# Two-layer graph network on 16 groups of four graphs: the first turn's convolution as 17 single taps, with a new opening order, and three moves inside the steps

## The chip, the cores and the metric

The kernel runs on one core of one Trainium2 chip. The metric is the device time of one execution in microseconds; the time before is the median of three runs. The profile is that of one further execution.

## The reference, cut to what matters

For 64 graphs of 128 nodes and 128 features:

```
h  = relu(layernorm(x))
# layer 0
c  = relu(bn1(conv1(hT)))                 # a 128x128 product, hT is [128 features, 128 nodes]
xc = relu(bn2(conv2(c)) + hT)             # 17 taps over the nodes, 128x128 each, zero pads of 8
s  = h @ w_se.T + b_se                    # 3 coordinates per node
A  = exp(-(|s_n|^2 + |s_m|^2 - 2 s_n.s_m))
nm = A @ relu(h @ w_msg.T + b_msg)
r, z, n: gates of [xc, nm] @ w_ih.T and h @ w_hh.T;  x = x + (1 - z) n + z h
# layer 1
x  = x + adj @ (relu(layernorm(x)) @ W) + b
```

Every product of layer 0's convolutions and gates is made as three products of numbers split into a high and a low part (high by high, high by low, low by high).

## The kernel before, in words

Four graphs are a group (512 columns), there are 16 groups, and two groups p and q are a turn, so there are 8 turns (NS). Each of the engines has its own list of instructions, written out by hand; they meet by semaphores. PE's list (L277 to L583) is `opening()`, then `step(t)` for t = 1 to 7, then `ending()`. A step finishes the state of the turn before (groups pp, qq: turned back by `o_turn`, second layernorm, `adj_h2`, `layer2`), does the convolution and the gates of its own turn (p, q), and does for the next turn (a, b) what lies ahead of a convolution: `x_turn` (transpose of the normalised x), `conv1`, `messages` (messages and the three coordinates), `rows_turn`, `distances`, `neighbour_sums`.

The second convolution (L284 `product`) is not made of 17 taps. The nodes are taken in four phases (node number modulo 4), and phases and taps are combined in sums and differences, so that for the four output phases nine products of four or five tap weights do. Each product is on 256 columns (8 graphs of 32 nodes), and each of its taps is three matmuls: 40 taps, 120 matmuls a turn. It needs sums of weights (M12, M22, M32, M21, M23; POOL L1190 to L1197), differences of phases (`pre`, POOL L825: five instructions into px), and sums of the results (`scaled_first`, `between`, `scaled_third`, POOL `sums` L1210: four instructions). `split_hi` (ACT L587) and `split_lo` (DVE L928) split the phases and their differences in five parts; `round_w` (ACT L592) and `split_w` (DVE L934) split the 37 tap weights in five parts, once.

Other helpers that the prediction speaks of: `hidden` (ACT L605) and `hidden_lo` (DVE L879) read the bank in which x was turned, and conv1 waits for them; `pairs` (DVE L885) copies the coordinates out of the bank of the messages (L890) and builds with eight or nine small instructions the rows that `rows_turn` transposes; `left_rows` (ACT) and `right_rows` (DVE L909) fill what `distances` multiplies; `decay`, `masked` (L919) give the attention; `conv_out`, `conv_round`, `conv_lo_out` finish the convolution for `gates_c`; `blend_start`, `candidate`, `blend_end` (L939 to L954) make the state that `o_turn` transposes; `residual` (L956) adds it to x; `normalise1`, `shift1` (L848), `scale1` (POOL L1151) and `first` (ACT L596) are the first layernorm of groups to come; `keep_clock(n)` (L299) issues n products of the identity that nobody reads.

In the order before, POOL's `opening()` waits for `pair_set` 4 (the last rows of coordinates of the first four groups) ahead of its five `pre` for turn 1 (L1235), and every step does the same (L1248).

Of the kernel before, what the change touches and what calls it, by code (L numbers as in the profile page):

```python
# [38 lines left out]
def gnn_kernel(nc, x_in, adj_in, vec_in, early_in, conv_in, gate_in, late_in, bias_in, out):  # L39
    ctx = ExitStack()  # L40
    with ctx:
# [68 lines left out]
        sv = sb("sv", [128, GG, S + 1])  # L110
# [115 lines left out]
        CX_FILLS = (0, 1, 2, 4, 4)  # L226

        def cx_source(k):
            return c1[:, 3:4] if k == 0 else px[:, CX_PARTS[k][0]:CX_PARTS[k][1]]

# [3 lines left out]
        def _(sp):  # L234
# [18 lines left out]
            load_x(4)  # L253
            for g in range(4, ARING):
                load_adj(g)
# [22 lines left out]
        def _(pe):  # L278
# [5 lines left out]
            def product(acc, side, x, weights):  # L284
# [5 lines left out]
                return last  # L290

# [161 lines left out]
            def opening():  # L453
                pe.wait_ge(ident_set, 1)
                keep_clock(17)
                x_turn(0)
                x_turn(1)
                keep_clock(9)
                conv1(0)
                conv1(1)  # L460
                messages(0)
                pe.wait_ge(w_split, 1)
                pe.wait_ge(cxlo_set, 1)
                product(pP, 0, X22, four(M22, True))
                messages(1)
                rows_turn(0)
                pe.wait_ge(w_split, 2)
                pe.wait_ge(cxlo_set, 2)
                product(pP, 1, X12, four(M12, True)).then_inc(f_done[0], 1)
                distances(0)  # L470
                rows_turn(1)
                pe.wait_ge(w_split, 3)
                product(pQ, 0, X21, four(M21, True))
                x_turn(2)
                distances(1)
                neighbour_sums(0)
                pe.wait_ge(cxlo_set, 3)
                product(pQ, 1, X23, four(M23)).then_inc(f_done[1], 1)
                conv1(2)
                messages(2)  # L480
                x_turn(3)
                neighbour_sums(1)
                pe.wait_ge(s1_set, 1)
                product(pP, 0, X32, four(M32)).then_inc(f_done[2], 1)
                conv1(3)
                messages(3)
                pe.wait_ge(w_split, 5)
                pe.wait_ge(cxlo_set, 5)
                pe.wait_ge(t_set, 1)
                product(pQ, 0, X11, four(A0, True))  # L490
                rows_turn(2)
                product(pQ, 1, X13, four(A2)).then_inc(f_done[3], 1)
                distances(2)
                pe.wait_ge(s32_set, 1)
                rows_turn(3)
                product(pP, 0, X31, four(A1))
                distances(3)
                neighbour_sums(2)
                product(pP, 1, X33, four(A3)).then_inc(f_done[4], 1)
                neighbour_sums(3)  # L500
                for g in range(2):
                    gates_h(g)
                    gates_n(g)
                    gates_c(g)

            def step(t):
                a, b, p, q, pp, qq = 2 * t + 2, 2 * t + 3, 2 * t, 2 * t + 1, 2 * t - 2, 2 * t - 1
                front, middle = t + 1 < NS, t < NS
                if front:
                    x_turn(a)  # L510
                o_turn(pp)
                if middle:
                    have(pe, cxlo_set, 5 * t + 1)
                    have(pe, ct_set, 2 * t)
                    product(pP, 0, X22, four(M22, True))
                if front:
                    conv1(a)
                    messages(a)
                    x_turn(b)
                if middle:  # L520
                    have(pe, cxlo_set, 5 * t + 2)
                    product(pP, 1, X12, four(M12, True)).then_inc(f_done[0], 1)
# [11 lines left out]
                if middle:  # L534
                    have(pe, cxlo_set, 5 * t + 3)
# [4 lines left out]
                if middle:  # L540
                    have(pe, s1_set, t + 1)
# [5 lines left out]
                if middle:  # L547
                    have(pe, cxlo_set, 5 * t + 5)
                    have(pe, t_set, t + 1)
                    product(pQ, 0, X11, four(A0, True))  # L550
# [5 lines left out]
                if middle:  # L556
                    have(pe, s32_set, t + 1)
# [28 lines left out]
        def _(act):  # L586
            def split_hi(t, k):  # L587
                have(act, c1_set if k == 0 else pre_set, 2 * t + 2 if k == 0 else 5 * t + CX_PRES[k])
                have(act, f_done[CX_FILLS[k]], t)
                act.activation(cx_hi[:, CX_PARTS[k][0]:CX_PARTS[k][1]], cx_source(k), ACT.Copy).then_inc(cxhi_set, 1)  # L590

# [19 lines left out]
            def conv1_out(g):  # L611
# [4 lines left out]
                if g % 2 == 0:  # L616
                    have(act, pre_set, 5 * (g // 2) - 2)
                    have(act, cxlo_set, 5 * (g // 2) - 4)
# [69 lines left out]
            def scaled_third(t):  # L688
                have(act, f_done[2], t + 1)
# [4 lines left out]
            def gates(t):  # L694
# [4 lines left out]
                if t + 1 < NS:  # L699
# [5 lines left out]
                if t == 0:  # L705
                    first(4)
                    first(5)
                hidden_gate(q)
                reset_gate(q)
                update_gate(q)  # L710

            def opening():
                act.dma_start(vec[:], vec_in).then_inc(vec_loaded, 16)
                act.dma_start(late[:], late_in).then_inc(late_loaded, 16)
# [8 lines left out]
                conv1_out(0)  # L723
                round_w(0)
                conv1_out(1)
                split_hi(0, 0)
                messages(0)
                round_w(1)
                split_hi(0, 1)
                left_rows(0)  # L730
                messages(1)
                round_w(2)
                decay(0)
# [576 lines left out]
```

## Time and profile before

| | us |
|---|---|
| median of three runs | 376.99 (376.59 to 378.67) |
| the profiled execution, its time | 378.42 |
| the profiled execution, its span | 376.5 |
| busy: PE / DVE / ACT / POOL | 341.2 / 286.4 / 208.7 / 174.1 |
| granted TensorE clock, mean | 0.964 |

In 40 slices of the span (9 is 90% busy or more; the clock in tenths of full):

```profile
PE   5758776979999999999999999999999999989864
DVE  4596688797878997797879887889767987653572
POOL 7763247212890179224951298118911594072022
PEclk9886889998999999999999999999999999999998
```

A slice is 9.4 us. The steps have regular length from slice 10 on; ahead of it lie the opening and the first step. A matmul's record is longer than the time until the next one starts, so what a stream of matmuls costs is read from their starts.

### The profile page before, as it was taken

Reading aid. Unit: us, or ns where it says so; the run is one execution under the profiler, and the core shown is the slowest. Engines: PE = TensorE matmul, PEld = TensorE weight load, DVE = VectorE, ACT = ScalarE, POOL = GpSimd, SP = SyncE. Lnnn points to the kernel's source line nnn. Section 1 sums busy time; section 2 is a strip of 40 time slices with the busy share of each in tenths; the row PEclk is TensorE's granted clock in tenths of the full one; section 3 lists DMA queues with packets and bytes.
Section 4 is the critical chain, followed back from the end, with each engine's and each line's share of the span. In section 5 each row is a group of like instructions: output and inputs, shape, how many; then the busy total and the mean of one; then the engine's idle time right before and its main releaser. Section 6 shows DMA issues by size and latency. Waiting matters only on the chain.

```text
span 376.5 us, 6337 instructions
## 1 busy us (share of the span) xinstructions
PE 341.2 (91%) x2212; PEld 311.8 (83%) x2212; DVE 286.4 (76%) x737; ACT 208.7 (55%) x403; POOL 174.1 (46%) x140
## 2 busy tenths in 40 slices
PE   5758776979999999999999999999999999989864
PEld 5757776769998899889988999889988998989663
DVE  4596688797878997797879887889767987653572
ACT  1545733576854686548744785468645835262242
POOL 7763247212890179224951298118911594072022
PEclk9886889998999999999999999999999999999998
DMA  7700020000220013000310031001100010000001
GB/s 256 275 3 0 0 66 20 0 1 2 86 83 2 1 58 113 0 0 30 105 36 1 2 112 57 0 2 65 49 1 2 0 57 1 3 28 30 0 0 57
DMA packets 7951, 15.10 MB, mean 40 GB/s; under 512 B 1008, under 2 KB 1648, under 8 KB 7792
## 3 DMA queue, kind: packets, MB, share of 16 engines
q1 hardware_dynamic: 7632, 14.56, 11.1%
q8 instruction: 18, 0.29, 0.3%
q10 hardware_dynamic: 288, 0.14, 0.1%
q14 instruction: 13, 0.11, 0.1%
HBM read 10.50 MB, written 4.19 MB: 39 GB/s over the span
## 4 chain that ended last, share of the span: by engine, by line
issue 40%; POOL 28%; PE 13%; DVE 11%; ACT 5%; DMA 1%; SPq 0%; POOLq 0%; DVEq 0%; ACTq 0%
POOL rs L1161 3%; POOL ac L838 3%; POOL px L842 3%; POOL base L1213 3%; POOL x_ring L1203 3%; POOL base L1215 3%; POOL px L832 3%; POOL px L840 2%; POOL px L835 2%; POOL base L1219 2%; POOL rs L1156 2%; ACT hn L601 1%; DMA x_ring<-x_in 1%; DVE cx_lo L931 1%; DVE st L855 1%
## 5 line engine op out<-in xcount | busy, mean ns | idle before, releaser
L1161 POOL TENSOR_TENSOR rs<-ve,neg_half 128x4 f32<-128x4 f32 x16 | 16.1, 1009 | 103.8 <-DVE ve L972 103.8
L280 PE MATMUL pP<-cx_hi,conv_hi 128*128 128x256 f32 x176 | 54.4, 309 | 5.6 <-DVE cx_lo L931 5.6
L281 PE MATMUL pP<-cx_lo,conv_hi 128*128 128x256 f32 x176 | 52.0, 296 | 0.0
L282 PE MATMUL pP<-cx_hi,conv_lo 128*128 128x256 f32 x176 | 52.0, 296 | 0.0
L280 PE MATMUL pQ<-cx_hi,conv_hi 128*128 128x256 f32 x144 | 46.0, 319 | 2.7 <-issue 2.2
L281 PE MATMUL pQ<-cx_lo,conv_hi 128*128 128x256 f32 x144 | 43.2, 300 | 0.0
L282 PE MATMUL pQ<-cx_hi,conv_lo 128*128 128x256 f32 x144 | 43.1, 299 | 0.0
L1156 POOL TENSOR_TENSOR rs<-ve,neg_half 128x8 f32<-128x8 f32 (+1 forms) x9 | 14.9, 1656 | 56.5 <-DVE ve L862 56.5
L280 PEld LDWEIGHTS pP<-cx_hi,conv_hi 128*128 128x128 f32 x176 | 34.4, 195 | 6.0 <-DVE conv_lo L936 3.5
L931 DVE TENSOR_TENSOR cx_lo<-px,cx_hi 128x576 fp32r<-128x576 f32 x32 | 35.0, 1116 | 0.6 <-ACT cx_hi L590 0.6
L282 PEld LDWEIGHTS pP<-cx_hi,conv_lo 128*128 128x128 f32 x176 | 34.3, 195 | 0.0
L281 PEld LDWEIGHTS pP<-cx_lo,conv_hi 128*128 128x128 f32 x176 | 34.3, 195 | 0.0
L280 PEld LDWEIGHTS pQ<-cx_hi,conv_hi 128*128 128x128 f32 x144 | 28.9, 201 | 3.5 <-issue 2.3
L649 ACT ACTIVATE work<-work,nb,rs 128x128 f32<-128x128 f32 x60 | 24.7, 482 | 10.5 <-DVE nb L976 10.5
L281 PEld LDWEIGHTS pQ<-cx_lo,conv_hi 128*128 128x128 f32 x144 | 28.9, 201 | 0.0
L282 PEld LDWEIGHTS pQ<-cx_hi,conv_lo 128*128 128x128 f32 x144 | 28.8, 200 | 0.0
L669 ACT ACTIVATE work<-pNR,rz_b 128x512 f32<-128x512 f32 x16 | 11.0, 686 | 31.2 <-PE pNR L282 31.2
L1203 POOL TENSOR_TENSOR x_ring<-work,late 128x512 f32<-128x512 f32 x16 | 23.0, 1440 | 11.2 <-DVE pair L907 11.2
L992 DVE SCALAR_TENSOR_TENSOR xc_lo<-base,xc_hi 128x512 fp32r<-128x512 f32 x16 | 17.1, 1066 | 12.1 <-ACT xc_hi L659 12.1
L942 DVE SCALAR_TENSOR_TENSOR work<-work 128x512 f32<-128x512 f32 x16 | 11.9, 744 | 17.1 <-ACT work L669 17.1
L922 DVE TENSOR_TENSOR att<-att,adj_ring 128x512 f32<-128x512 f32 x16 | 23.1, 1445 | 2.2 <-ACT att L640 1.8
L601 ACT ACTIVATE hn<-x_ring,nb,rs 128x128 f32<-128x128 f32 x56 | 22.3, 481 | 0.7 <-DVE nb L868 0.7
(246 smaller groups left out, 1022.3 us busy)
## 6 DMA issues: line engine op xcount, KB each, us to landing
x_ring<-x_in SPq DMA_DIRECT2D x16, 256.0 KB, 2.6
adj_ring<-adj_in SPq DMA_DIRECT2D x16, 256.0 KB, 3.3
out<-x_ring SPq DMA_DIRECT2D x15, 256.0 KB, 2.0
work<-conv_in SPq DMA_DIRECT2D x1, 1088.0 KB, 7.5
x_ring<-gate_in SPq DMA_DIRECT2D x1, 576.0 KB, 7.9
out<-x_ring SPq DMA_DIRECT2D x2, 128.0 KB, 1.7
work<-bias_in SPq DMA_DIRECT2D x1, 132.0 KB, 7.4
early<-early_in SPq DMA_DIRECT2D x1, 129.5 KB, 2.9
```

The source lines that it names most:

```text
L280: pe.matmul(acc, w_hi, m_hi, start=start, stop=False)
L281: pe.matmul(acc, w_hi, m_lo, start=False, stop=False)
L282: return pe.matmul(acc, w_lo, m_hi, start=False, stop=stop)
L601: last = act.activation(graph(hn[g % 2], j), xs(g, j), ACT.Identity, bias=nb1[:, i:i + 1], scale=rs1[:, i:i + 1])
L649: last = act.activation(graph(h2[g % 2], j), graph(x1[g % 2], j), ACT.Relu, bias=nb2[g % 2][:, j:j + 1], scale=rs2[g % 2][:, j:j + 1])
L922: dve.tensor_tensor(att[g % 2], att[g % 2], adjs(g), ALU.mult).then_inc(att_set, 1)
L931: dve.tensor_tensor(cx_lo[:, part], cx_source(k), cx_hi[:, part].bitcast(F32), ALU.subtract)\
L942: dve.scalar_tensor_tensor(cand[g % 2], tr, 1.0, cand[g % 2], ALU.add, ALU.mult).then_inc(rh_set, 1)
L992: dve.scalar_tensor_tensor(xc_lo[:, 2 * e:2 * e + 2], base[e][:], 0.0, xc_hi[:, 2 * e:2 * e + 2].bitcast(F32), ALU.max, ALU.subtract)\
L1156: pool.tensor_tensor(rs1[:, lane], ve1[:, lane], neg_half[:, lane], ALU.pow).then_inc(rs1_set, 1)
L1161: pool.tensor_tensor(rs2[g % 2][:], ve2[g % 2][:], neg_half[:, 0:GG], ALU.pow).then_inc(rs2_set, 1)
L1203: pool.tensor_tensor(xs(g).rearrange("p (g d) -> p g d", g=GG), x1[g % 2].rearrange("p (g d) -> p g d", g=GG), l1_bias, ALU.add).then_inc( ...
```

## The change

What it does:

1. **The first turn's convolution** is made by `direct(tap)`: 17 single taps on the split phases themselves. The high and low phases are stored in the order 0, 2, 1, 3 (SLOT), so that two phases are one operand of 512 columns where they lie side by side, and two of 256 where they don't. For turn 0 this drops the nine products, POOL's five `pre` and four `sums`, ACT's five `split_hi`, two `scaled_first` and `scaled_third`, DVE's five `split_lo` and `between`. It adds two `split_hi_phases`, two `residual_phases` (ACT) and two `split_lo_phases` (DVE). POOL's sums of weights move behind `scale1([2, 3])`, the weights are split in six parts with the plain taps first, and turn 1's parts are split in the order 0, 3, 4, 1, 2.
2. **The opening's lists** of all four engines and the loads' order are new. `pairs` is cut in `coordinates` (the copy out of the bank, into one of two sv) and `pair_rows` (the rest). POOL no longer waits for `pair_set` 4 ahead of turn 1's `pre`.
3. **In the steps**: `x_turn` of the next turn's first group moves from the step's start into q's gates (between `gates_h(q)` and `gates_n(q)`), with `hidden` and `hidden_lo`; `o_turn(p)` moves between `gates_n(q)` and `gates_c(q)`, with `residual(p)` ahead of `normalise1` on DVE; `x_turn(b)` moves ahead of `conv1(a)`; part 2 of the next turn's phases is split in the gates; POOL's `sums` move ahead of `with_bias(qq)` and of `pre` 2 and 3.

The diff outside the opening, cut to its core:

```diff
-        W_PARTS = (taps(5, T16), taps(8, M12), taps(8, M21), taps(8, A0), taps(8, A2))
-        W_SUMS = (2, 2, 3, 0, 0)
+        W_PARTS = (taps(8, A0), taps(8, A2), taps(1, T16), taps(4, M22), taps(8, M12), taps(8, M21))
+        W_SUMS = (0, 0, 0, 2, 2, 3)
...
+        FIRST_ORDER = (0, 3, 4, 1, 2)
+
+        SLOT = (0, 2, 1, 3)
...
             load_x(0)
+            load_x(1)
             sp.dma_start(early[:], early_in).then_inc(early_loaded, 16)
-            load_x(1)
...
             load_x(4)
+            sp.dma_start(late[:], late_in).then_inc(late_loaded, 16)
...
+            def direct(tap, start=False, stop=False):
+                w = T16 if tap == 16 else 4 * (tap % 4) + tap // 4
+                w_hi, w_lo = conv_hi[:, w * D:(w + 1) * D], conv_lo[:, w * D:(w + 1) * D]
+                ends = []
+                for e, bank in enumerate((pQ, pP)):
+                    at_even, at_odd = e + tap, e + 2 + tap
+                    slots = [SLOT[at_even % 4], SLOT[at_odd % 4]]
+                    if slots[1] == slots[0] + 1 and at_even // 4 == at_odd // 4:
+                        parts = [(bank[:], slice(slots[0], slots[0] + 2), at_even // 4)]
+                    else:
+                        parts = [(bank[:, 0:CG * QN], slice(slots[0], slots[0] + 1), at_even // 4),
+                                 (bank[:, CG * QN:], slice(slots[1], slots[1] + 1), at_odd // 4)]
+                    for acc, phases, at in parts:
+                        m_hi, m_lo = cx_hi[:, phases, :, at:at + QN], cx_lo[:, phases, :, at:at + QN]
+                        ends.append((pe.matmul(acc, w_hi, m_hi, start=start, stop=False),
+                                     pe.matmul(acc, w_hi, m_lo, start=False, stop=False),
+                                     pe.matmul(acc, w_lo, m_hi, start=False, stop=stop)))
+                return ends
...
-                if front:
-                    x_turn(a)
-                o_turn(pp)
...
                 if front:
+                    x_turn(b)
                     conv1(a)
                     messages(a)
-                    x_turn(b)
...
                     gates_h(q)
+                    if t + 2 < NS:
+                        x_turn(a + 2)
                     if not front:
                         o_turn(p)
                     gates_n(q)
+                    if front:
+                        o_turn(p)
                     gates_c(q)
...
+            def residual_phases(e):
+                act.wait_ge(hT_set, 2)
+                act.activation(base[e][:], own(0, e), ACT.Identity, bias=bn_b[:, 1:2]).then_inc((sumE_set, sumO_set)[e], 1)
...
                 hidden_gate(q)
+                if t + 2 < NS:
+                    hidden(p + 4)
                 reset_gate(q)
...
+                if 0 < t < NS - 1:
+                    split_lo(t + 1, 2)
                     split_lo(t + 1, 3)
                     split_lo(t + 1, 4)
                 blend_start(p)
...
                 blend_end(p)
+                if t + 2 < NS:
+                    hidden_lo(p + 4)
+                if t + 1 < NS:
+                    residual(p)
                 if t + 3 < NS:
                     normalise1([p + 6, p + 7])
...
                 blend_start(qq)
-                if front:
-                    hidden_lo(a)
-                residual(pp)
                 blend_end(qq)
+                normalise2(pp)
+                if front:
+                    coordinates(a)
+                    hidden_lo(b)
+                    pair_rows(a)
```

The opening after the change, engine by engine, with the calls joined on lines. PE:

```
keep_clock(15); x_turn(0); keep_clock(3); x_turn(1); conv1(0); conv1(1); messages(0); keep_clock(6)
wait w_split 1, cxlo_set 2
direct(0); direct(4); direct(8); messages(1); direct(12); direct(1); direct(5); rows_turn(0)
direct(9); x_turn(2); direct(13); rows_turn(1); distances(0)
wait w_split 2
direct(2); conv1(2); distances(1); messages(2); x_turn(3); direct(6); neighbour_sums(0)
direct(10); conv1(3); neighbour_sums(1); direct(14); messages(3); rows_turn(2); direct(3)
distances(2); direct(7); rows_turn(3); direct(11); distances(3); neighbour_sums(2); direct(15)
wait w_split 3
direct(16); gates_h(0); neighbour_sums(3); gates_n(0); gates_c(0)
gates_h(1); x_turn(4); gates_n(1); o_turn(0); gates_c(1)
```

ACT, from `conv1_out(0)` on:

```
conv1_out(0); round_w(0); conv1_out(1); split_hi_phases(0); split_hi_phases(1); round_w(1); round_w(2)
messages(0); residual_phases(0); messages(1); residual_phases(1); gate_hi; first(2); left_rows(0)
hidden(2); first(3); left_rows(1); decay(0); round_w(3); conv1_out(2); round_w(4); hidden(3)
decay(1); sums_hi(0); messages(2); round_w(5); conv1_out(3); sums_hi(1); messages(3)
left_rows(2); decay(2); split_hi(1, 0); split_hi(1, 3); left_rows(3); split_hi(1, 4); decay(3)
sums_hi(2); conv_round(0, 0); hidden_gate(0); conv_round(0, 1); first(4); sums_hi(3)
reset_gate(0); update_gate(0); candidate(0); split_hi(1, 1); split_hi(1, 2)
hidden_gate(1); hidden(4); first(5); reset_gate(1); update_gate(1)
```

DVE, from `split_w(0)` on:

```
split_w(0); split_lo_phases(0); split_lo_phases(1); coordinates(0); split_w(1); normalise1([2, 3])
split_w(2); pair_rows(0); coordinates(1); shift1([2, 3]); pair_rows(1); right_rows(0)
hidden_lo(2); right_rows(1); masked(0); split_w(3); coordinates(2); split_w(4); hidden_lo(3)
masked(1); pair_rows(2); sums_lo(0); gate_lo; split_w(5); coordinates(3); right_rows(2)
sums_lo(1); pair_rows(3); masked(2); right_rows(3); normalise1([4, 5]); masked(3); sums_lo(2)
conv_out(0, 0); shift1([4, 5]); split_lo(1, 0); conv_lo_out(0, 0); conv_out(0, 1)
split_lo(1, 3); conv_lo_out(0, 1); sums_lo(3); split_lo(1, 4); blend_start(0)
split_lo(1, 1); split_lo(1, 2); blend_end(0); hidden_lo(4); residual(0); normalise1([6, 7])
```

POOL: `scale1([0])` and `scale1([1])` are moved between the small instructions of the biases, so that the sums of weights lie behind them:

```
wait cxlo_set 2; scale1([2, 3]); the three sums of weights; pre(1, 1) to pre(1, 5); scale1([4, 5])
```

## Rows read from the trace of the kernel before

**Rows 1.** Stages, all engines: window, its length, busy us of each engine, clock, DMA.

```profile
19.80:78.46 58.66, 46.51 (x258) 41.38 (x259) 47.45 (x118) 31.51 (x59) 23.21 (x15) 0.85 0.05 14
78.46:121.98 43.52, 40.96 (x270) 37.72 (x269) 35.70 (x105) 27.44 (x55) 21.04 (x15) 0.96 0.11 38
202.98:243.49 40.51, 39.82 (x269) 36.55 (x268) 33.53 (x91) 25.50 (x50) 20.50 (x15) 1.00 0.12 40
```

**Rows 2.** Waits of PE between 17.1 and 79.2 us: total, times, longest.

```profile
PE pP L280 <- DVE cx_lo L931: 5.6, 2, 3.3
```

**Rows 3.** Stages at the lower clock, same columns as rows 1.

```profile
25.20:35.50 10.30, 7.51 (x31) 6.68 (x32) 9.16 (x18) 4.48 (x10) 6.10 (x4) 0.51 0.01 2
42.30:45.70 3.40, 3.40 (x18) 3.40 (x17) 2.14 (x4) 1.68 (x4) 1.28 (x1) 0.51 0.00 0
52.50:56.00 3.50, 3.50 (x19) 3.50 (x18) 2.80 (x12) 0.87 (x2) 0.73 (x1) 0.52 0.45 137
83.30:86.70 3.40, 2.75 (x10) 2.50 (x11) 3.25 (x13) 0.78 (x1) 0.00 (x0) 0.50 0.02 5
```

**Rows 4.** Waits of PE, first 79.2 to 125 us, then 125 to 324 us.

```profile
PE pH L280 <- DVE h_lo L882: 2.6, 1, 2.6
...
PE pH L280 <- issue: 1.8, 5, 0.4
PE pH L280 <- DVE h_lo L882: 1.5, 5, 0.3
```

**Rows 5.** PE in order of time: start, us, line, shape: 256 columns, then 512.

```profile
20.61 0.30 PE L280 MATMUL pP<-cx_hi,conv_hi 128*128 128x256 f32 x1
20.75 0.30 PE L281 MATMUL pP<-cx_lo,conv_hi 128*128 128x256 f32 x1
...
67.10 0.40 PE L280 MATMUL pZ<-h_hi,gate_hi 128*128 128x512 f32 x1
67.33 0.40 PE L281 MATMUL pZ<-h_lo,gate_hi 128*128 128x512 f32 x1
```

**Rows 6.** DVE, then PE, in order of time, up to the first product.

```profile
12.49 0.69 DVE L882 SCALAR_TENSOR_TENSOR h_lo<-pI,h_hi 128x512 fp32r<-128x512 f32 x1 [0.34 <-ACT hT L609]
...
14.43 0.77 PE L280 MATMUL pH<-h_hi,early_hi 128*128 128x512 f32 x1
...
19.80 0.36 PE L280 MATMUL pP<-cx_hi,conv_hi 128*128 128x256 f32 x1 [2.30 <-DVE cx_lo L931]
```

**Rows 7.** DVE's groups by line over the whole span: ns min/median/max.

```profile
L936 DVE TENSOR_TENSOR conv_lo<-work,conv_hi x5: 824/1218/1560, 17.2 to 42.4; 128x1024 fp32r<-128x1024 f32 x4, 128x640 fp32r<-128x640 f32 x1
...
L931 DVE TENSOR_TENSOR cx_lo<-px,cx_hi x32: 748/758/1967, 25.6 to 315.9; 128x576 fp32r<-128x576 f32 x32
```

**Rows 8.** DVE (first three), then POOL, in order of time.

```profile
46.38 0.69 DVE L892 TENSOR_TENSOR sq<-sv 128x12 f32<-128x12 f32 x1
...
47.31 1.02 DVE L896 CAST svx<-sv 128x16 fp32r<-128x16 f32 x1
...
48.91 0.17 DVE L907 COPY pair<-svx 128x8 f32<-128x8 f32 x1
...
45.75 1.29 POOL L1215 TENSOR_TENSOR base<-base,s 128x512 f32<-128x512 f32 x1
47.00 1.29 POOL L1219 TENSOR_TENSOR base<-base,hT 128x512 f32<-128x512 f32 x1
...
57.99 1.88 POOL L838 TENSOR_TENSOR ac<-c 128x576 f32<-128x576 f32 x1
```

**Rows 9.** DVE, then PE, in order of time, around the start of step 4.

```profile
199.83 1.64 DVE L855 BATCH_NORM_STATS2 st<-x_ring 128x6 f32<-128x128 f32 x8
...
202.57 0.69 DVE L942 SCALAR_TENSOR_TENSOR work<-work 128x512 f32<-128x512 f32 x1 [0.22 <-ACT work L669]
...
213.69 0.69 DVE L914 TENSOR_TENSOR right<-pF,vec 64x512 fp32r<-64x512 f32 x1
...
215.39 0.39 PE L374 MATMUL pF<-right,left 128*128 128x512 f32 x1
```

More of the change, by code:

```diff
@@ L109, in gnn_kernel @@
         sq = sb("sq", [128, GG, S])
-        sv = sb("sv", [128, GG, S + 1])
+        sv = [sb(f"sv{i}", [128, GG, S + 1]) for i in range(2)]
         svx = sb("svx", [128, GG, 2, S + 1], F32R)
@@ L461, in opening @@
                 messages(0)
+                keep_clock(6)
                 pe.wait_ge(w_split, 1)
-                pe.wait_ge(cxlo_set, 1)
-                product(pP, 0, X22, four(M22, True))
+                pe.wait_ge(cxlo_set, 2)
+                direct(0, start=True)
+                direct(4)
+                direct(8)
                 messages(1)
+                direct(12)
+                direct(1)
+                direct(5)
                 rows_turn(0)
-                pe.wait_ge(w_split, 2)
@@ L468, in opening @@
[L468 to L474, printed above, removed]
+                direct(9)
+                x_turn(2)
+                direct(13)
+                rows_turn(1)
+                distances(0)
+                pe.wait_ge(w_split, 2)
+                direct(2)
@@ L475, in opening @@
+                conv1(2)
                 distances(1)
[L476 to L479, printed above, removed]
                 messages(2)
                 x_turn(3)
+                direct(6)
+                neighbour_sums(0)
+                direct(10)
+                conv1(3)
                 neighbour_sums(1)
-                pe.wait_ge(s1_set, 1)
-                product(pP, 0, X32, four(M32)).then_inc(f_done[2], 1)
@@ L485, in opening @@
[L485 removed]
+                direct(14)
                 messages(3)
[L487 to L490, printed above, removed]
                 rows_turn(2)
[L492 removed]
+                direct(3)
                 distances(2)
[L494 removed]
+                direct(7)
                 rows_turn(3)
[L496 removed]
+                direct(11)
@@ L497, in opening @@
                 distances(3)
                 neighbour_sums(2)
-                product(pP, 1, X33, four(A3)).then_inc(f_done[4], 1)
-                neighbour_sums(3)
[L501 to L504, printed above, removed]
+                direct(15)
+                pe.wait_ge(w_split, 3)
+                even, odd = direct(16, stop=True)
+                even[2].then_inc(f_done[3], 1)
+                odd[0].then_inc(f_done[0], 1)
@@ L506, in step @@
+                odd[1].then_inc(f_done[1], 1)
+                odd[2].then_inc(f_done[4], 1)
+                gates_h(0)
+                neighbour_sums(3)
+                gates_n(0)
+                gates_c(0)
+                gates_h(1)
+                x_turn(4)
+                gates_n(1)
+                o_turn(0)
+                gates_c(1)
             def step(t):
@@ L1251, in step @@
                     pre(pool, t + 1, 1)
-                    pre(pool, t + 1, 2)
+                if middle:
+                    sums(t)
                 with_bias(qq)
                 if front:
-                    pre(pool, t + 1, 3)
-                if middle:
-                    sums(t)
-                if front:
-                    pre(pool, t + 1, 4)
-                    pre(pool, t + 1, 5)
+                    for k in range(2, 6):
+                        pre(pool, t + 1, k)
             def ending():
```

264 lines of the change are left out of this document (144 added, 120 removed).

## The prediction, made before the changed kernel was run

> **What bounds the kernel now.** I read the stages first [rows 1]. Cut at the starts of `x_turn(a)`, a regular step lasts 40.51 us and PE is busy for 39.82 of it: PE's list of matmuls is the bound there, and only 0.69 us are waits. These are two waits of conv1 on the split of the turned x, 3.3 us in the five steps 2 to 6 [rows 4]. The first step lasts 43.52, 3.0 more than a regular one: one such wait of 2.6 [rows 4], and 3.4 us of half clock [rows 3]. The 58.66 us from the first product to the end of the first turn's gates are different: PE is busy for 46.51 and idle for 12.15, and 2.30 more of idle lie ahead of the first product [rows 1, 6]. The largest waits are two, together 5.6, on the low part of the phases, which comes last of the chain conv1, c1, POOL's differences, ACT's high part, DVE's low part [rows 2]. What the idle time costs is more than its length: the granted clock is at half (1.2 of 2.4 GHz) for three stretches, in which PE is busy for 7.51 + 3.40 + 3.50 = 14.4 us, half of which, 7.2, would not be there at the full one [rows 3]. So the opening holds 14.45 us of idle and 7.2 of low clock, and all seven steps hold 3.3 + 3.7 and a little more. That is what can be won.
>
> **Part 1, more matmuls.** At full clock a matmul of 256 columns starts 0.13 us after the last, one of 512 columns 0.233 [rows 5]. The nine products are 120 x 0.13 = 15.6 us. Of the 17 taps, each on two banks, I count from SLOT 18 bank-taps with phases side by side and 16 without: 18 x 3 = 54 matmuls of 512 columns, 12.6 us, and 16 x 6 = 96 of 256, 12.5 us; together 25.1. **The change adds 9.5 us of PE.** The rest of PE's work in the turn comes from the busy time: 46.51 - 7.2 (low clock) - 15.6 - 54 gate matmuls x 0.233 (12.6) = 11.1, and x_turn(4) and o_turn(0), which now lie inside, add 0.8. New sum: 25.1 + 12.6 + 11.9 = 49.6 us without waits, at full clock.
>
> **The start.** conv1(0) began at 14.43 behind nine pairs of keep_clock, though what conv1(1) needs last was ready at 13.18 [rows 6]; with three pairs ahead of x_turn(1), conv1(1) follows the latter and ends near 13.9. Then ACT: c1 0.8, the two copies of 576 elements 1.2 together; DVE: two subtractions, the second 0.76 [rows 7] after the last copy: 16.8, and some 0.3 less because x(1) is loaded second. Bounds: no gain by the load, 17.1; the whole gain of landing as early as the third of the loads, 15.8. I take 16.5, against 19.80 before [rows 6]. The weights' first eight taps need no sum and are split (1.05 and 1.22 [rows 7]) ahead of the copies' end.
>
> **What can make PE wait.** I walked the four new lists with the durations of the trace. DVE has 35 us of work from split_w(0) (near 14) to sums_lo(3): 37 taps of weights 5.7, two phase parts 1.5, `normalise1` twice 4.8 [rows 9], `pair_rows` four times 7, `right_rows`, `hidden_lo`, `masked`, `sums_lo` at 0.65 each, gate_lo 1.3. Undisturbed it ends at 50 to 52 where PE comes to gates_c(0) near 56, so DVE has little to spare, and POOL disturbs it. The trace shows how: sq, an instruction of 0.17 us, took 0.69 and ended with POOL's instruction (45.75 + 1.29); the next copy took 1.02 and ended with POOL's next one (47.00 + 1.29), while all of them together need 1.7 us when POOL is still [rows 8]. The median split of 576 elements takes 0.76, the slowest 1.97 [rows 7]. Before, POOL waited for `pair_set` 4; now it runs its five `pre` (1.3 to 1.9 each [rows 8], 7.9 in all) as soon as c1 of groups 2 and 3 is there, at 40.7 in my walk, behind gate_lo from 41.7 on. Then split_w(5) waits for pre 1, and in pair_rows(3) sq waits for pre 3, the copy for pre 4, the next one for pre 5: ready at 51.6, while PE comes to rows_turn(3) at 47.2. **A wait of 4.4 us.** The smaller ones are 0.5 at distances(0) (the same with the sums of weights, 6.2 us on POOL beside pair_rows(1)), 0.5 at distances(2), 0.5 at o_turn(0), which waits for blend_end(0). Sum 5.9. For the clock I take one stretch of 3.4 us behind the wait of 4.4 (1.7 lost) and half a stretch at the start (0.8): 2.5. Bounds: no wait and no low clock, 0; as much as before, 14.5 + 7.2.
>
> Sum of part 1: 16.5 + 49.6 + 5.9 + 2.5 = 74.5 as the start of step 1's first product; before it was at 78.46 + 0.8 = 79.3. **4.8 us gained.** What is dropped on ACT (five copies, three scalings) and on POOL (nine instructions) cost time before only through the waits counted above, so it is not counted again. `late` on the SP queue lands well ahead of layer 2; the x loads 5 to 7 wait for gate_lo, which comes 10 us earlier.
>
> **Part 3, step 1.** The wait of 2.6 and its low clock go, since h of group 4 is split in the gates before: 3.0 + 0.7 (its share of the regular waits), less the wait of part 4: 3.7 - 0.95 = 2.7 gained.
>
> **Part 4, steps 2 to 6.** Nothing is added to PE. The two waits go (0.69). What is late next: DVE. Before, `normalise1` filled the hole between blend_end(p) and the tanh of q's reset gate, from 199.83 to 202.35, and blend_start(q) began at 202.57 [rows 9]. Now hidden_lo(a) and residual(p) lie ahead of it, and residual waits for o_turn(p), which PE reaches at 201.2 and ends at 201.6: `normalise1` runs from 202.4 to 204.8, and blend_start(q), which could begin at 203.3, begins 1.5 later. Behind it in DVE's list are the second normalise, hidden_lo(b), pair_rows(a), right_rows(a). By the walk hidden_lo(b) is ready at 210.7 where PE wants it at 210.2 (0.5), and right_rows(a) at 215.15 where PE wants distances(a) at 214.7 (0.45); before, it was ready at 214.38 for 215.39, 1.0 to spare [rows 9]. So 0.95 in place of 0.69, 0.25 lost in each of steps 2 to 5: -1.0. From turn 5 on there is no `normalise1` in the gates: step 6 gains its 0.6, step 7 (o_turn(12) and residual(12) earlier) 0.3. Bounds of a step: 0.69 gained, 2.4 + 0.6 lost if DVE's lag reached PE whole. POOL's sums come 5 us earlier, `pre` 5 1 us later, at about the time of the copies: no cost. The tail from 364 us on is the same.
>
> **Sum.** 4.8 + 2.7 - 1.0 + 0.9 = 7.4 us. Against the profiled execution's own time, 378.42 (span 376.5 and 1.9 around it), that is 371.0; it stands 1.4 above the median, so against the median 376.99 it is 369.6. Since my DVE walk puts each block at its full length, I take 369.
>
> **Rivals.**
> A, the cover holds: POOL and DVE block each other less, PE waits 1 us and the clock stays up in the opening, and the steps lose their waits. Opening 79.3 - (16.5 + 49.6 + 1) = 12.2, step 1 3.7, steps 2 to 6 3.4, step 7 0.3: 19.6, so 357.4; with one third of the waits left, 362. For it: POOL idles in most of the first 60 us [rows 1], and DVE and POOL queue up only where both have work. Against: DVE's busy share is 81% already in that stage [rows 1].
> B, DVE becomes the opening's bound: all of POOL's 18.7 us (two scales, sums of weights, `pre`) are added to DVE's 35: 14 + 35 + 18.7 = 67.7 for the last split that gates_c(0) needs, then 12.6 + 1.5 - 4.2 of gates left: 77.6. Gain 1.7 + 2.7 - 0.1 = 4.3, so 372.7. Rows 8 speak for the mechanism, but not all of DVE's instructions are blocked: right_rows took 0.69 in the middle of a step [rows 9].
> The Trainium skill ("SBUF — State Buffer", SBUF: two separate sides) says that VectorE and GpSimd share a port pair under an exclusive lock, held for the whole instruction, by VectorE instructions with two SBUF inputs or in a two-port mode; it speaks against this change, and taken for every instruction it would be rival B's 372.7.
> C, slower: DVE's lag in the gates lands on PE in each of steps 1 to 5. Its place is `normalise1` behind residual(p); its price at most 2.4 + 0.6 + what is not won (0.7) = 3.7 a step; it decides from 1.5 a step on, where it eats the 7.4. At 2.8 a step it is 369 + 5 x 2.8 less the 1.3 already counted, 381.7. For it: DVE's instructions are stretched to 2.0 us in the steps too [rows 7]. Against: the 1.0 us to spare at distances [rows 9].
> D, the taps bring nothing: the 9.5 us of PE are paid and the waits stay beyond half: 376 to 379.
>
> **Chances.** Forecast (365 to 372.5) 0.46, A 0.25, B 0.13, C 0.07, D 0.09. The range holds A from 359 on, the forecast, B and half of D: 359 to 376.5. About 0.5% is what a measurement of this kernel can tell from no change (1.9 us: 375.1 to 378.9). Faster: forecast, A, B and a little of D, 0.85; same 0.08; slower 0.07.
>
> **What would show it.** Right: the first wide product of a tap near 16.5; the turn's gates end near 74; one long PE wait at rows_turn(3), released by DVE's pair rows, which are stretched beside POOL's px; the steps within 0.3 of 40.5, with waits on h_lo and `right` in steps 2 to 5 and none in step 6. Wrong: steps of 39.8 (A), PE waiting throughout the opening for DVE (B), steps over 42 (C), clock at half for over 10 us before 75 (D).

## The result, and the profile of the changed kernel

The changed kernel takes 367.42 us (median of four runs, 366.19 to 367.97), the kernel before 376.97: a ratio of 0.974 (95% interval 0.970 to 0.978), 2.6% faster. I had forecast 369, between 359 and 376.5. The profiled execution has a span of 366.2 us, against 376.5.

The stages of the changed kernel, in the columns of [rows 1]. The first is the whole first turn from its first tap to the first product of step 1, then steps 1, 2, 4, 6 and 7, cut at their first product or at the end of the gates ahead of it, then the tail:

```profile
15.90:70.63 54.73, 51.83 (x297) 44.96 (x298) 44.19 (x118) 31.13 (x60) 17.52 (x10) 0.97 0.06 18
70.63:111.41 40.78, 39.86 (x270) 36.54 (x269) 32.46 (x91) 25.48 (x50) 20.30 (x14) 1.00 0.13 40
111.41:152.41 41.00, 39.86 (x270) 36.53 (x268) 32.50 (x91) 25.48 (x50) 20.28 (x14) 1.00 0.12 40
...
192.90:233.64 40.74, 39.87 (x269) 36.53 (x268) 32.57 (x91) 25.46 (x50) 20.32 (x14) 1.00 0.12 40
...
274.63:313.50 38.87, 38.87 (x265) 36.02 (x264) 29.55 (x72) 21.42 (x40) 18.24 (x13) 1.00 0.04 14
313.50:348.69 35.19, 32.83 (x215) 29.80 (x214) 18.55 (x49) 12.57 (x23) 11.32 (x10) 1.00 0.05 16
348.69:366.20 17.51, 10.27 (x53) 9.19 (x51) 7.54 (x20) 6.02 (x13) 2.79 (x3) 0.71 0.08 30
```

For the kernel before, steps 6 and 7 between the same points:

```profile
284.79:324.77 39.98, 39.37 (x267) 36.11 (x265) 31.44 (x73) 21.97 (x43) 18.94 (x13) 1.00 0.04 14
324.77:360.30 35.53, 33.25 (x221) 30.27 (x220) 19.20 (x49) 12.63 (x24) 11.63 (x10) 1.00 0.04 15
```

So the 10.3 us between the two spans come from these places:

| stage | before | after | gained | forecast |
|---|---|---|---|---|
| up to the first product or tap | 19.80 | 15.90 | 3.9 | 3.3 |
| from there to step 1's first product | 59.45 | 54.73 | 4.7 | 1.5 |
| step 1 | 43.51 | 40.78 | 2.7 | 2.7 |
| steps 2 to 5 | 162.0 | 163.2 | -1.2 | -1.0 |
| step 6 | 39.98 | 38.87 | 1.1 | 0.6 |
| step 7 | 35.53 | 35.19 | 0.3 | 0.3 |
| tail | 16.2 | 17.5 | -1.3 | 0 |

PE's waits, over 12 to 71 us and then over the steps (total, times, longest):

```profile
PE pF L401 <- DVE pair L980: 2.5, 1, 2.5
PE pQ L322 <- DVE cx_lo L1003: 0.9, 1, 0.9
PE pQ L296 <- DVE h_lo L949: 0.5, 1, 0.5
PE pH L470 <- DVE work L1032: 0.4, 1, 0.4
...
PE pF L409 <- ACT left L694: 3.6, 5, 0.9
PE pZ L477 <- ACT work L708: 1.3, 1, 1.3
PE pH L296 <- DVE h_lo L949: 1.0, 5, 0.2
PE pH L470 <- DVE work L1032: 1.0, 1, 1.0
```

Of the first four rows the second and third lie ahead of the first tap. Of the last four, the waits at L409 and L296 are those of steps 1 to 5 and the other two those of step 7.

The 12.15 us of idle that the first turn had [rows 1] have become 2.9, and of the three stretches of half clock [rows 3] one is left, behind the one long wait. So 9.2 us of waits and 5.5 of low clock are gone, against 9.5 of added matmuls and 0.5 of other work: the 4.7 of the table. No run keeps the nine products in the new order of the lists, so how much of this the single taps gained and how much the order is not shown. The long wait is where the forecast had it: `rows_turn(3)` (L401) waits for the pair rows of the fourth group:

```profile
48.45 0.33 PE L401 MATMUL pF<-ident,pair 128*128 128x128 f32 x1 [2.49 <-DVE pair L980]
```

This is DVE in order of time, with POOL's third and fifth `pre` (ac and px) beside it:

```profile
44.13 0.89 DVE L965 TENSOR_TENSOR sq<-sv 128x12 f32<-128x12 f32 x1
...
45.26 1.26 DVE L969 CAST svx<-sv 128x16 fp32r<-128x16 f32 x1
46.55 1.30 DVE L971 TENSOR_TENSOR svx<-sv,svx 128x16 fp32r<-128x16 f32 x1
...
48.23 0.17 DVE L980 COPY pair<-svx 128x8 f32<-128x8 f32 x1
...
43.57 1.42 POOL L905 TENSOR_TENSOR ac<-c 128x576 f32<-128x576 f32 x1
...
46.45 1.38 POOL L909 TENSOR_TENSOR px<-ac,px 128x560 f32<-128x560 f32 x1
```

Three instructions of 0.17 us each end with an instruction of POOL (44.99, 46.5, 47.83), and the group takes 4.3 us. The walk had 1.7 for it with POOL still.

The clock stretch in the first turn:

```profile
49.70:53.10 3.40, 3.40 (x15) 3.01 (x15) 3.07 (x19) 0.69 (x2) 0.75 (x1) 0.54 0.00 0
```

### The profile page after: what moved, and what is told of

Read it like the earlier page. It is cut to its first block, busy times and chain, and to the rows that moved or that the text cites. A ratio compares the mean times of both kernels' runs of the same rounds, so it can differ in the third digit from the quotient of the medians.

```text
span 366.2 us, 6363 instructions
## 1 busy us (share of the span) xinstructions
PE 344.8 (94%) x2238; PEld 312.9 (85%) x2238; DVE 271.2 (74%) x734; ACT 207.5 (57%) x400; POOL 158.2 (43%) x131
## 4 chain that ended last, share of the span: by engine, by line
issue 41%; POOL 27%; PE 19%; DVE 7%; ACT 3%; DMA 1%; POOLq 0%; DVEq 0%; ACTq 0%
POOL rs L1249 4%; POOL px L909 3%; POOL base L1303 3%; POOL rs L1244 3%; POOL base L1306 3%; POOL px L899 2%; POOL ac L905 2%; POOL px L902 2%; POOL x_ring L1291 2%; POOL base L1297 2%; PE pQ L322 1%; PE pP L322 1%; PE pP L323 1%; PE pP L324 1%; PE pQ L324 1%
## 5 line engine op out<-in xcount | busy, mean ns | idle before, releaser
L296 PE MATMUL pP<-cx_hi,conv_hi 128*128 128x256 f32 x154 | 46.4, 301 | 0.0
L298 PE MATMUL pP<-cx_hi,conv_lo 128*128 128x256 f32 x154 | 45.0, 292 | 0.0
L297 PE MATMUL pP<-cx_lo,conv_hi 128*128 128x256 f32 x154 | 45.0, 292 | 0.0
L296 PE MATMUL pQ<-cx_hi,conv_hi 128*128 128x256 f32 x126 | 39.0, 309 | 0.0
L298 PE MATMUL pQ<-cx_hi,conv_lo 128*128 128x256 f32 x126 | 36.8, 292 | 0.0
L297 PE MATMUL pQ<-cx_lo,conv_hi 128*128 128x256 f32 x126 | 36.8, 292 | 0.0
L296 PEld LDWEIGHTS pP<-cx_hi,conv_hi 128*128 128x128 f32 x154 | 29.4, 191 | 0.3
L1291 POOL TENSOR_TENSOR x_ring<-work,late 128x512 f32<-128x512 f32 x16 | 22.8, 1423 | 11.1 <-DVE pair L980 11.1
L1009 DVE TENSOR_TENSOR cx_lo<-px,cx_hi 128x576 fp32r<-128x576 f32 x28 | 26.4, 982 | 0.8 <-ACT cx_hi L641 0.8
L296 PEld LDWEIGHTS pQ<-cx_hi,conv_hi 128*128 128x128 f32 x126 | 24.1, 192 | 0.0
L718 ACT ACTIVATE xc_hi<-base 128x512 fp32r<-128x512 f32 x16 | 10.1, 631 | 18.3 <-DVE base L1065 18.3
L641 ACT ACTIVATE cx_hi<-px 128x576 fp32r<-128x576 f32 x28 | 17.6, 674 | 4.8 <-POOL px L899 3.7
```

The lines of the kernel that those rows point to most:

```text
L296: pe.matmul(acc, w_hi, m_hi, start=start, stop=False)
L297: pe.matmul(acc, w_hi, m_lo, start=False, stop=False)
L298: return pe.matmul(acc, w_lo, m_hi, start=False, stop=stop)
L1009: dve.tensor_tensor(cx_lo[:, part], cx_source(k), cx_hi[:, part].bitcast(F32), ALU.subtract)\
L1291: pool.tensor_tensor(xs(g).rearrange("p (g d) -> p g d", g=GG), x1[g % 2].rearrange("p (g d) -> p g d", g=GG), l1_bias, ALU.add).then_inc( ...
```

## The experiments

Each is the changed kernel with the edit shown. Times are medians of four runs; the runs were made in three sets on three chips, on which the kernel before read between 377.5 and 378.6, so ratios to it are given, and versions of different sets are compared by them. "Step 1 begins" is the start of its first product (70.63 above), which ends the opening and the first turn.

**The changed kernel again.** No edit.

> The changed kernel itself once more, on the chip of the next three, to compare with: 366 to 368 us, regular steps of 40.74, first product of step 1 at 70.6.

Measured: 367.25 us, 0.970 of before (0.969 to 0.972). Step 1 begins at 70.48, the steps are the same to 0.04 us. The span is 365.1: the tail is 1.0 us shorter than in the first profile, and the difference comes from the clock:

```profile
348.56:365.10 16.54, 8.24 (x53) 7.47 (x51) 8.62 (x20) 6.02 (x13) 2.79 (x3) 0.90 0.09 32
```

The eight-fold products of L477 and L485 ran at full clock here and ended 1.8 us earlier in the tail. The next wait of PE (L345) was 1.1 us longer, 2.8 against 1.8: a small DVE instruction ahead of it (L1054) now met one of POOL (L1291), ended with it and took 1.22 us in place of 0.15.

So 1.0 of the 1.3 us that the tail lost is no part of the change: executions of one kernel differ in it.

### The steps

**Turns of x and of the state back at the steps' start.**

```diff
+                if t > 1:
+                    if front:
+                        x_turn(a)
+                    o_turn(pp)
...
-                    if t + 2 < NS:
-                        x_turn(a + 2)
...
-                    if front:
-                        o_turn(p)
...
-                if t + 2 < NS:
-                    hidden_lo(p + 4)
-                if t + 1 < NS:
-                    residual(p)
                 if t + 3 < NS:
                     normalise1([p + 6, p + 7])
```

`hidden`, `hidden_lo` and `residual` are at the steps' start again too.

> The changed kernel with one part undone: in steps 2 to 7 x_turn of the turn's first group and o_turn of the finished one are at the step's start again, with hidden, hidden_lo and residual there; step 1 and the opening stay as changed. Theory (the moves inside q's gates cost, since normalise1 stands behind residual): regular steps fall from 40.75 to about 40.3 to 40.5 us, step 6 rises from 38.9 to about 39.9, the whole changes by -1.5 to +0.5 us. Rival (the moves are what gains in the steps): steps of 41.3 or more, the whole 3 us or more slower.

Measured: 363.23 us, 0.961 (0.960 to 0.963). A regular step takes 39.63 us without a wait of PE. The direction is that of the theory and the size is not: undoing this part gains 1.1 us a step against the changed kernel, and 0.9 against the kernel before, whose waits I had expected to come back. Step 6 rose only to 39.1, not to 39.9. Something else in the change had removed those.

**normalise1 ahead of hidden_lo and residual.**

```diff
+                if t + 3 < NS:
+                    normalise1([p + 6, p + 7])
                 if t + 2 < NS:
                     hidden_lo(p + 4)
                 if t + 1 < NS:
                     residual(p)
-                if t + 3 < NS:
-                    normalise1([p + 6, p + 7])
```

> The changed kernel with normalise1 ahead of hidden_lo and residual in the gates, the opening's too; nothing else. Theory (normalise1 behind residual delays blend_start of q by 1.3 us, and everything behind it on DVE and, through shift2 and second, on ACT): both waits of PE in steps 1 to 5 go, a regular step takes 39.4 to 39.6 us, the whole is 5.5 to 7 us faster than the changed kernel (about 361). Rival 1 (distances waits for ACT's left rows because of ACT's own list): only the wait on h_lo goes, 0.4 us a step, 2 us in all. Rival 2 (hidden_lo comes too late for conv1(a)): no gain or a loss.

Measured: 361.03 us, 0.955 (0.953 to 0.958), 5.6 us under the changed kernel by the two ratios. Steps 3 to 5 take 39.31, step 1 takes 40.54 with one wait of 0.7 for the left rows. The step of the two kernels (the same as 192.90:233.64 above) in which the turns are at the start, and in which they are in the gates behind normalise1:

```profile
189.71:229.34 39.63, 39.63 (x269) 36.56 (x268) 32.54 (x91) 25.35 (x50) 19.95 (x15) 1.00 0.13 41
```

```profile
189.68:228.99 39.31, 39.31 (x270) 36.44 (x268) 32.61 (x91) 25.58 (x50) 19.97 (x15) 1.00 0.13 42
```

The move of the turns is good for 0.3 us a step, and the place of normalise1 cost 1.4. Rival 1 is refuted as the whole cause, since both waits went with ACT's list as it was: ACT's left rows came late because `second`, ahead of them, waits for DVE's shift2, which was behind normalise1.

**left_rows(a) ahead on ACT.**

```diff
                 second(pp)
+                if front:
+                    left_rows(a)
                 if middle:
                     scaled_first(t)
                 if front:
                     conv1_out(b)
-                    left_rows(a)
```

> The changed kernel with left_rows(a) ahead of scaled_first and conv1_out(b) in ACT's list of a step; nothing else. Theory: distances(a) waits for ACT's left rows by ACT's order, and DVE's right rows come only 0.6 us ahead of them; so the wait of 0.68 falls to 0 to 0.2 and the step from 40.74 to about 40.0, 3 to 4 us in all. Rival (right rows, behind normalise1 on DVE, are the bound at once): the wait keeps its length and is put down to DVE; no gain.

Measured: 364.11 us, 0.962 (0.959 to 0.965), 3.1 under the changed kernel. The step falls to 40.24, and the wait, now for DVE's right rows, to 1.3 us in five:

```profile
PE pF L409 <- DVE right L988: 1.3, 5, 0.4
```

So ACT's list was the last of two causes that stand 0.5 us apart, and both lead back to DVE, as the run before this one shows.

**x_turn(b) back behind messages(a), turns at the start.**

```diff
                 if front:
-                    x_turn(b)
                     conv1(a)
                     messages(a)
+                    x_turn(b)
```

On ACT `hidden(b)` moves behind `messages(a)` with it, as before the change.

> The changed kernel with the turns of x and of the state back at the steps' start (as in e1_turns_back) and, besides, x_turn(b) behind messages(a) again. It asks what made e1's steps 39.63 us where those of before took 40.51. Theory (x_turn(b) ahead of conv1(a), which gives hidden and hidden_lo of b time): regular steps rise by 0.5 us or more, with a wait of conv1 on h_lo of 0.2 to 0.4 again. Rival (the copy of the coordinates ahead of hidden_lo(b), or POOL's order): under 0.2 a step.

Measured: 373.45 us, 0.989 (0.984 to 0.995); a step 41.37, 1.74 more than with x_turn(b) early. Three waits are back, the two on the turned x and the one on the left rows:

```profile
PE pF L409 <- ACT left L694: 4.2, 6, 0.9
PE pH L296 <- DVE h_lo L949: 3.2, 6, 1.9
PE pH L296 <- issue: 1.8, 5, 0.4
```

This is a part that the prediction does not weigh: turning b's x before conv1(a) instead of after messages(a) is what makes conv1(b) find its input, and without it the new steps are 0.9 us slower than the old ones (41.37 against 40.51).

**The copy of the coordinates back with the rest, turns at the start.**

```diff
                 if front:
-                    coordinates(a)
-                    hidden_lo(b)
-                    pair_rows(a)
+                    pairs(a)
+                    hidden_lo(b)
```

> The changed kernel with the turns back at the steps' start (as in e1_turns_back) and, besides, the copy of a's coordinates no longer apart: all of a's pair rows ahead of hidden_lo(b) on DVE. Theory: 1.3 us later for hidden_lo(b), but conv1(b) has more than that to spare with x_turn(b) early: steps within 0.1 of 39.63. Rival (the order of the copies is what gained): 0.3 us a step or more lost, with a wait on h_lo.

Measured: 365.39 us, 0.966 (0.962 to 0.970); a step 40.07, 0.44 more, with the wait on h_lo back. The theory is refuted: there was not 1.3 us to spare.

```profile
190.60:230.67 40.07, 39.73 (x270) 36.54 (x268) 32.22 (x91) 25.47 (x50) 20.00 (x15) 1.00 0.13 41
```

### The opening

**POOL's five pre held until the pair rows are built.**

```diff
                 sum_phases()
+                pool.wait_ge(pair_set, 4)
                 for k in range(1, 6):
...
-                split_hi(1, 3)
                 left_rows(3)
-                split_hi(1, 4)
                 decay(3)
                 sums_hi(2)
+                split_hi(1, 3)
+                split_hi(1, 4)
```

> The changed kernel, with POOL's five pre of turn 1 held until the pair rows of the fourth group are built (as before the change), and ACT's splits of parts 3 and 4 behind left_rows(3), decay(3) and sums_hi(2) so that they do not hold them up. Theory (DVE's pair rows are blocked by POOL's pre): pair_rows(3) takes 1.7 instead of 4.3 us, the PE wait of 2.5 at rows_turn(3) falls under 0.3, the stretch of half clock behind it goes, and the opening ends 3.5 to 4.8 us earlier. Rival (DVE is simply late there by the amount of its work): the wait stays above 1.5. Other rival: the pre come too late for the splits and a wait of 1 us or more appears ahead of gates_c(0) or step 1's products.

Measured: 366.24 us, 0.969 (0.967 to 0.971). The pair rows are built from 44.30 to 45.6, and the wait at rows_turn(3) and the half clock are gone:

```profile
44.30 0.16 DVE L965 TENSOR_TENSOR sq<-sv 128x12 f32<-128x12 f32 x1
...
45.46 0.17 DVE L980 COPY pair<-svx 128x8 f32<-128x8 f32 x1
```

So the block by POOL is shown. But step 1 begins at 69.13, only 1.4 us earlier than in the repeated run of the changed kernel and not the 3.5 to 4.8 of the theory. One wait has come at gates_c(0), as the second rival has it, and the one at o_turn(0) has grown from 0.4 (PE's in order of time):

```profile
58.40 0.50 PE L296 MATMUL pNR<-xc_hi,gate_hi 128*128 128x512 f32 x1 [1.55 <-DVE xc_lo L1070]
66.53 0.66 PE L470 MATMUL pH<-ident,work 128*128 128x128 f32 x4 [1.15 <-DVE work L1032]
```

**POOL's pre held only from the third on.** ACT's order as in the last run.

```diff
                 for k in range(1, 6):
+                    if k == 3:
+                        pool.wait_ge(pair_set, 4)
                     pre(pool, 1, k)
```

> The changed kernel with POOL's wait for the pair rows of the fourth group only ahead of pre 3 (pre 1 and 2 run before they are built), and ACT's order as in the run with all five held. Theory: no DVE instruction of pair_rows(3) is blocked, and the px parts come 2 to 3 us earlier than with all five held; neither the wait of 2.5 at rows_turn(3) nor the one of 1.5 at gates_c(0) is there, no half clock before 300 us, first product of step 1 at 66 to 67.5. Rival: another wait takes their place (blend_end(0) at o_turn(0), by the splits ahead of it), 68.5 or later.

Measured: 363.2 us, 0.959 (0.958 to 0.961), 4.1 under the changed kernel. Step 1 begins at 66.53, within the theory's 66 to 67.5, the pair rows are built in 1.3 us, and of the opening's waits the long one is gone and no new one has come:

```profile
PE pQ L322 <- DVE cx_lo L1003: 0.9, 1, 0.9
PE pQ L296 <- DVE h_lo L949: 0.5, 1, 0.5
PE pH L470 <- DVE work L1032: 0.4, 1, 0.4
```

**A third of the taps' work left out.** The low-by-high product of taps 0 to 15 of the first turn is missing, 7.9 us of PE.

```diff
                         ends.append((pe.matmul(acc, w_hi, m_hi, start=start, stop=False),
-                                     pe.matmul(acc, w_hi, m_lo, start=False, stop=False),
-                                     pe.matmul(acc, w_lo, m_hi, start=False, stop=stop)))
+                                     pe.matmul(acc, w_hi, m_lo, start=False, stop=False)))
+                        if stop:
+                            ends[-1] += (pe.matmul(acc, w_lo, m_hi, start=False, stop=True),)
```

> The changed kernel, with the low-by-high product left out of taps 0 to 15 of the first turn (16 wide and 32 narrow matmuls, 7.9 us of PE); that part of the computation is missing. If PE alone bounds the opening outside of its counted waits, the first turn's gates end about 7.9 us earlier. If DVE and ACT stand close behind it, as my walk of the lists has them, the waits grow and only 2 to 5 us of it come out. If they bound it, under 1.

Measured: 365.11 us, 0.967 (0.965 to 0.968). Step 1 begins at 67.93, 2.6 us earlier than in the repeated run of the changed kernel. Two thirds of the 7.9 us taken from PE did not come out; the waits between the first tap and step 1 have grown from 2.9 to 7.4 us:

```profile
PE pF L402 <- DVE pair L981: 3.6, 1, 3.6
PE pF L410 <- ACT left L695: 1.0, 1, 1.0
PE pF L366 <- ACT hn L661: 1.0, 1, 1.0
PE pI L402 <- DVE pair L981: 0.9, 1, 0.9
PE pZ L410 <- DVE right L988: 0.5, 1, 0.5
```

This suggests that most of the 9.5 us that the single taps add to PE lie in time that DVE and ACT need there anyway.

**x(1) loaded third again.**

```diff
-            load_x(1)
             sp.dma_start(early[:], early_in).then_inc(early_loaded, 16)
+            load_x(1)
```

> The changed kernel with x(1) the third load again, behind the first weights. Theory: x(1) lands at about 6.9 in place of 4.9 us, the first tap starts 1.2 to 2.0 us later than 15.90, and the first product of step 1 comes later by 0.5 to the same amount, since DVE, which is nearly the bound, is late by it as a whole. Rival: the opening's later waits swallow it, under 0.3.

Measured: 368.95 us, 0.975 (0.971 to 0.980). DVE reads x(1) from 6.07 us on, against 4.88, and not from 6.9. The first tap starts at 17.04, 1.14 later. Step 1 begins at 70.27, which looks earlier than 70.48, but this execution has no half clock in the first turn, as two others whose openings have no edit (left_rows ahead, 69.19; x_turn(b) back, 69.32). Against these it is 1.0 later: the later start comes through nearly whole. The interval overlaps that of the changed kernel; by the whole time alone it could not be told.

### Together

**normalise1 ahead, left_rows(a) ahead, POOL held from pre 3 on.** The three edits above.

> The changed kernel with normalise1 ahead in the gates, left_rows(a) ahead on ACT, and POOL's wait ahead of pre 3: the candidate that beats both. If the three gains add up: first product of step 1 at 66 to 67.5, steps of 39.3, the whole 10 to 12 us under the changed kernel, 356 to 358. If they share a cause, more than 358.5.

Measured: 356.65 us, 0.942 (0.940 to 0.944), 10.6 us under the changed kernel. Step 1 begins at 66.58 and takes 40.05 us, and each of steps 2 to 5 takes 39.31:

```profile
185.01:224.32 39.31, 39.31 (x270) 36.43 (x268) 32.62 (x91) 25.67 (x50) 19.98 (x15) 1.00 0.13 42
```

**And idle products in the ending.**

```diff
                 adj_h2(END - 1)
+                keep_clock(4)
                 layer2(END - 1)
+                keep_clock(8)
                 end_pass(0)
```

> The best kernel so far (e10_all_three) with 4 and 8 pairs of idle products in the ending ahead of layer2(14) and of the last group's pass, on the theory that the half clock of the last 10 us, which some executions have, costs 1 us there. If they keep the clock up: 0.5 to 1 us faster than 356.6. If they stand in the way, or the clock falls all the same: equal or up to 1 us slower.

Measured: 355.4 us, 0.9405 (0.937 to 0.945). The last 16 to 17 us of the two kernels:

```profile
338.00:355.00 17.00, 9.79 (x53) 8.72 (x51) 7.48 (x20) 6.02 (x13) 2.71 (x3) 0.64 0.09 31
```

```profile
338.10:354.10 16.00, 11.18 (x77) 10.25 (x75) 7.50 (x20) 6.02 (x13) 2.75 (x3) 0.89 0.09 33
```

The tail is 1.0 us shorter at a mean clock of 0.89 instead of 0.64. The four executions of this kernel had a mean clock of 0.995 to 1.0 over the whole span, those of the kernel without the idle products 0.983 to 0.990. But a tail without them can reach 0.90 as well (16.54 us, in the repeated run of the changed kernel). The two were not run on the same chip, and their intervals overlap; that the whole gains by it is likely and not shown.

## Why the prediction was right, point by point

**The number.** The stages gained 10.3 us where the sum had 7.4: part 1 gave 3.8 more, the tail took 1.3, the steps gave 0.3 more. That the medians lie only 1.6 us from the forecast (367.42, 369) is in part luck: the profile of before stood 1.4 us above its median, that of the changed kernel 0.6, and the forecast had been set 0.6 below its own sum without a figure for it.

**The bound.** Right: the steps are PE's list plus small waits, the opening before was held back by waits and low clock. The run with a third of the taps' work left out shows DVE and ACT close behind PE in the opening.

**More matmuls.** The 49.6 us without waits at full clock came out: 54.73 less 2.9 of waits and 1.7 for one stretch of half clock (counted as in the forecast, as half of its 3.40 us) is 50.1.

**The start.** 16.5 forecast, 15.90 measured. x(1) landed by 4.9 us, near the early end of my bounds; loading it third costs 1.1.

**Waits and clock of the opening.** This is the term of part 1 that was mis-sized, "Sum 5.9" for the waits, which measured 2.9: 2.5 at rows_turn(3), where I had 4.4, 0.4 at o_turn(0), none at distances(0) and distances(2). The mechanism was right, with three instructions blocked as foretold. What was wrong is "split_w(5) waits for pre 1": split_w(5) (L1014) went first and took its usual 1.22 us, and it was pre 1 (L899) that was long:

```profile
39.76 1.22 DVE L1014 TENSOR_TENSOR conv_lo<-work,conv_hi 128x1024 fp32r<-128x1024 f32 x1
39.92 2.33 POOL L899 TENSOR_TENSOR px<-c 128x576 f32<-128x576 f32 x1 [12.53 <-ACT c L679]
```

The five pre took the 7.9 us foretold but began at 39.9, not at 41.7. So the rows were ready at 48.4 where the prediction had 51.6, and PE came for them at 46.0 where it had 47.2: two errors of 3.2 and 1.2 us that partly cancel. Step 1's first product was forecast for 74.5 and came at 70.6. The stretch of half clock behind the wait came as forecast, the half one at the start did not. Of the 3.8 us that part 1 gave beyond my 4.8, 0.6 are the start, 3.0 the waits, and the rest the clock, with 0.5 of other work against it.

**Steps 1 to 5.** The sum was right to 0.2 us, but by two errors that cancel, and one of its two parts had the wrong reason. distances(a) waited for the left rows, not for the right rows as I had it (they were there 0.5 us sooner). Both are late by normalise1, which was the step's mechanism and is shown by the run that moves it. What the prediction failed to see is that it was weighing two things at once: the earlier x_turn(b) and the earlier copy of the coordinates gained, and the place of normalise1 lost. Both terms were too small by about half a us a step: the place of normalise1 cost 1.4 (40.74 against 39.31) where it had 0.95, and the waits of before were worth 1.2 (40.51 against 39.31) where it had 0.69, for it counted each wait by its idle time. That the net of 0.25 a step came out, 0.23, is luck. The order of POOL's sums and the earlier split of part 2 were not run apart.

**Step 6.** 1.1 instead of 0.6: a wait costs more than its idle time (below), and both waits went there.

**The tail.** "The same" did not hold for this execution; 1.0 us of the 1.3 is clock that differs between executions, 0.3 is open.

**The rivals.** A (357.4) asked for 1 us of waits and full clock in the opening, and for no waits in the steps. The changed kernel is not it; the kernel with all three edits comes near it, at 356.65. B and C did not happen. C's place, normalise1 behind residual(p), was the right one and its price 1.4 a step, just under the 1.5 from which it decides; but the other moves in the steps paid 1.2 of it back (40.51 - 39.31), which I had not credited to them. The lock that the Trainium skill states ("SBUF — State Buffer", SBUF: two separate sides), held for a whole instruction against VectorE instructions with two SBUF inputs or in a two-port mode, agrees with the trace: the three blocked instructions of the pair rows read SBUF alone. `right_rows`, with one operand in PSUM, was not stretched: it took 0.69 us from 42.80 on, in the middle of POOL's pre 2 (42.22 to 43.62). Taken for every instruction, the lock would have been rival B, 5 us off. D is refuted.

## What to carry to other kernels

Where a step is bound by one engine's list and still has short waits, look on the other engines for work without a deadline that stands ahead of work with one: here 2.4 us of statistics for groups two turns ahead cost 5.6 us in all, behind an instruction that itself waited for PE. Two engines that block each other are best kept apart by a wait at the right place, not the safest one: with ACT's two splits moved back in both, holding all of POOL's five instructions gained nothing beyond the clock (step 1 at 69.1 against 69.2), and holding the last three gained 2.7 us. And when an edit bundles several moves, undo them one by one: two of these gained and one lost, and the sum showed almost nothing: a regular step went from 40.51 to 40.74.

## What the runs showed of the hardware

A wait of PE cost more here than the idle time that the profile gives it. PE in order of time, changed kernel, in step 5 with a wait of 0.19 and in step 6 without:

```profile
239.94 0.60 PE L470 MATMUL pI<-ident,work 128*128 128x128 f32 x4
...
240.73 0.50 PE L296 MATMUL pH<-h_hi,early_hi 128*128 128x512 f32 x1 [0.19 <-DVE h_lo L949]
...
280.67 0.60 PE L470 MATMUL pI<-ident,work 128*128 128x128 f32 x4
...
281.02 0.48 PE L296 MATMUL pH<-h_hi,early_hi 128*128 128x512 f32 x1
```

0.79 us between the same two starts, against 0.35: the wait of 0.19 costs 0.44, since the records of matmuls overlap and a wait is counted only from the end of the last one. The steps say the same: 0.87 us of waits in a step cost 40.74 - 39.31 = 1.4.

The half clock of one stretch of 3.4 us in the first turn depends on the execution, not only on the kernel: with the same wait of 2.5 us ahead of it, five profiles of kernels with the same PE list up to there have it and step 1 begins at 70.3 to 70.6; two do not, at 69.2 and 69.3. It costs about 1.2 us. None of the four profiles without that wait has it.
